# A router with experts and a Mamba scan on one core: softplus in two functions, the first low rows sent sooner, and a tile of one B product made by GpSimd

## The reference

```python
# layer 0: a router picks 2 of 4 experts for each pixel
logits = tokens @ router_w.T + router_b;  gates = softmax of the two largest
out = sum(gates[e] * (gelu(tokens @ fc1_w[e].T + fc1_b[e]) @ fc2_w[e].T + fc2_b[e]));  x = x + scale * out
# layer 1: LayerNorm over channels, then the same Mamba block on the 4096 pixels forwards and backwards
xr, z = split(x_norm @ W_in);  xr = silu(causal_conv4(xr) + conv_b)       # 192 channels
dbl = xr @ W_xproj;  dt = softplus(dbl[:6] @ W_dt + b_dt);  B, C = dbl[6:22], dbl[22:38]
h = exp(dt * A) * h + (dt * xr) * B;  y = sum_n(h * C)                    # 192 x 16 states, step by step
y = (y + xr * D) * silu(z);  out = (y_fwd + y_rev) @ W_out * 0.5 + x
```

## Time and profile before

| | before |
|---|---|
| median of 3 runs | 5707.55 us |
| profiled execution | 5689.39 us, of which the span on the core is 5687.6 us |
| granted TensorE clock, mean | 0.821 |
| VectorE, GpSimd, TensorE, ScalarE busy | 92%, 90%, 79%, 78% of the span |
| scans | 3072, the first at 218.1 us |
| a pair of bodies in the middle images | forward 84.8 us, reverse 86.2 us |

### The profile page before, as it was taken

How to read it: one execution, slowest core, us unless ns; L and a number is a source line. 1 busy time by engine, 2 the same in 40 slices (tenths; PEclk the granted TensorE clock), 3 DMA queues, 4 the chain that set the end, 5 groups by cost and what they waited for, 6 DMA issues and landing times.

```text
span 5687.6 us, 47285 instructions
## 1 busy us (share of the span) xinstructions
PE 4485.6 (79%) x12946; PEld 1323.8 (23%) x12946; DVE 5245.5 (92%) x4449; ACT 4435.3 (78%) x6737; POOL 5145.4 (90%) x2121
## 2 busy tenths in 40 slices
PE   8777887778877888778887788777887788876676
PEld 3222222222222222222222222222222222221121
DVE  2699999999999999999999999999999999999998
ACT  3578888888888878878888888888888888887675
POOL 0499999999999999999999999999999999999998
PEclk8887887788887888888887788887888788887777
DMA  4476777677776777776777777676777777776776
GB/s 112 112 176 166 174 178 168 164 175 174 170 178 162 170 176 174 167 176 165 173 175 166 170 177 172 167 178 162 173 179 166 171 173 170 173 173 160 173 174 153
DMA packets 417569, 954.68 MB, mean 168 GB/s; under 512 B 56624, under 2 KB 56873, under 8 KB 382744
## 3 DMA queue, kind: packets, MB, share of 16 engines
q1 hardware_dynamic: 417304, 951.65, 70.4%
HBM read 770.08 MB, written 181.36 MB: 167 GB/s over the span
## 4 chain that ended last, share of the span: by engine, by line
POOL 27%; DVE 18%; PE 17%; ACT 14%; DMA 12%; issue 9%; SPq 2%; POOLq 0%; DVEq 0%; ACTq 0%
POOL X L1467 17%; DVE X L1361 13%; POOL X L1458 8%; PE ps L747 4%; DVE X L1345 4%; PE ps L726 4%; ACT ps L1079 4%; DMA bc_d<-bc 3%; PE ps L781 3%; DMA lo_d<-bc 2%; DMA lo<-lo_d 2%; DMA out<-xf 2%; DMA hi_d<-S 2%; DMA xf<-x_d 1%; DVE hid L1325 1%
## 5 line engine op out<-in xcount | busy, mean ns | idle before, releaser
L1467 POOL TENSOR_TENSOR X<-X,cR 128x2048 f32<-128x2048 f32 x768 | 3477.8, 4528 | 61.8
L1361 DVE TENSOR_TENSOR_SCAN X<-ps,carry,X 128x512 f32<-128x512 f32 x2688 | 3262.6, 1263 | 137.4 <-ACT ps L1079 136.3
L1079 ACT ACTIVATE ps<-hi,amat 128x512 f32<-128x512 f32 x2048 | 1377.3, 682 | 672.9 <-DVE X L1361 668.8
L781 PE MATMUL ps<-X,red 128*32 128x512 f32 x6144 | 911.1, 671 | 486.8 <-POOL X L1467 486.2
L1458 POOL TENSOR_TENSOR X<-lo,bR 128x2048 f32<-128x2048 f32 x258 | 1167.8, 4527 | 68.9 <-DMA lo<-lo_d 68.2
L1345 DVE TENSOR_TENSOR X<-hi,ps 128x2048 f32<-128x2048 f32 x512 | 1159.8, 2265 | 49.1 <-PE ps L781 49.0
L747 PE MATMUL ps<-win,w_u 97*128 97x512 f32 (+1 forms) x2080 | 1159.3, 710 | 2.9 <-ACT xr L1034 0.9
L1079 ACT ACTIVATE ps<-lo,amat 128x512 f32<-128x512 f32 x1026 | 687.3, 677 | 121.5 <-DVE X L1361 104.3
L762 PE MATMUL ps<-xr,wd 128*96 128x512 f32 (+1 forms) x520 | 432.1, 928 | 276.0 <-ACT xr L1034 218.9
L747 PEld LDWEIGHTS ps<-win,w_u 97*128 97x128 f32 (+1 forms) x2080 | 390.0, 198 | 693.5 <-issue 690.5
L1361 DVE TENSOR_TENSOR_SCAN X<-ps,X 128x512 f32<-128x512 f32 x384 | 445.5, 1205 | 47.0 <-ACT ps L1079 36.5
(11 more groups left out here) (125 smaller groups left out, 3969.2 us busy)
## 6 DMA issues: line engine op xcount, KB each, us to landing
hi<-hi_d SPq DMA_DIRECT2D x516, 512.0 KB, 8.2
bR<-bc_d SPq DMA_DIRECT2D x516, 256.0 KB, 4.6
cR<-bc_d SPq DMA_DIRECT2D x516, 256.0 KB, 7.3
lo<-lo_d SPq DMA_DIRECT2D x516, 256.0 KB, 4.6
hi_d<-S SPq DMA_DIRECT2D x258, 256.0 KB, 8.3
y_d<-yf SPq DMA_DIRECT2D x128, 256.0 KB, 10.4
yb<-y_d SPq DMA_DIRECT2D x112, 256.0 KB, 9.9
win<-xn_d SPq DMA_DIRECT2D x130, 195.1 KB
```

The source lines that it names most:

```text
L781: last = mm(p_y[GRP * j:GRP * j + GRP, :], red[:, :], X[:, slot(par, s), j, :], start=False, stop=(s in (LOW - 1, NB - 1)), skip_group_che ...
L1079: A_(p_a[i % RING][:, :], dt, ACT.Exp, scale=amat[:, column(i):column(i) + 1]).then_inc(s_exp, 1)
L1361: V.tensor_tensor_scan(h, a, h, 0.0 if head else carry[:, i:i + 1], ALU.mult, ALU.add).then_inc(s_scan, 1)
L1467: G.tensor_tensor(batch(par, s), batch(par, s), quads(cR, par, s), ALU.mult).then_inc(s_hc, 1)
```

## The change

1. **Softplus in two functions.** ScalarE makes Exp(x) from PSUM and then Ln(1 + e). Abs is gone. `make_dt` takes max(x, min(Ln, 17.5)). ScalarE does Exp and Ln of the low rows at tile 0, the copy of B and C and Exp of the high rows at tile 1, Ln of the high rows at tile 2. VectorE does `make_dt` at tiles 3 and 5.
2. **Prologue.** SyncE sends B and C rows, B loads, low store and low loads ahead of the piece's store and the C loads. VectorE does the two `make_dt` between `gate_hidden` tiles. GpSimd does the two low products of body 0 ahead of `normalise`.
3. **A shared batch.** In even bodies and in reverse bodies the third high product (batch 4) is VectorE's for three tiles, and GpSimd makes the fourth, between `normalise` and `times_c` 3. The scan of tile 19 waits for it.

```diff
+        SHARED = LOW + 2
+        def shared(odd, rev):
+            return rev == 1 or not odd
...
             for j in range(LAST):
-                store_x2(0, j, j, PROLOGUE.by[f"p{j}"])
                 if j == AT_D0:
                     store_bc(0, 0)
                     load_b(0, 0)
-                    load_c(0)
                     store_low(0, 0)
                     load_low(0, 0)
+                store_x2(0, j, j, PROLOGUE.by[f"p{j}"])
+                if j == AT_D0:
+                    load_c(0)
                     store_high(0, 0)
                     load_high(0, 0)
...
-                A_(LOG[k], begin(u, f"D{k}")[0:ROWS_OF[k], :], ACT.Abs).then_inc(s_sp[k], 1)
-                act.wait_ge(s_sp[k], b * 3 + 1)
-                A_(LOG[k], LOG[k], ACT.Exp, scale=-1.0).then_inc(s_sp[k], 1)
+                A_(LOG[k], begin(u, f"D{k}")[0:ROWS_OF[k], :], ACT.Exp).then_inc(s_sp[k], 1)
...
+                    if i == 0:
+                        softplus_log(1, n + 1)
                     if i == 1:
                         copy_bc(u, n + 1)
-                        softplus_log(1, n + 1)
-                    if i == 2:
                         softplus_start(0, u, n + 1)
-                    if i == 3:
+                    if i == 2:
                         softplus_log(0, n + 1)
...
+                tiles = BATCH - (s == SHARED and shared(par, rev))
-                V.tensor_tensor(X[:, slot(par, s), :, :], hi[:, par, HIGH:2 * HIGH, :],
-                                p_b[:, :].unsqueeze(1).to_broadcast([P, BATCH, CH]), ALU.mult).then_inc(s_bh, 1)
+                V.tensor_tensor(X[:, slot(par, s), 0:tiles, :], hi[:, par, HIGH:HIGH + tiles, :],
+                                p_b[:, :].unsqueeze(1).to_broadcast([P, tiles, CH]), ALU.mult).then_inc(s_bh, 1)
...
+                if s == SHARED and j == BATCH - 1 and shared(par, rev):
+                    dve.wait_ge(s_bq, quarters(n))
...
-                    if i == 4:
+                    if i == 3:
                         make_dt(1, u, n + 1)
+                    if i == 5:
+                        make_dt(0, u, n + 1)
                     if i == 6:
-                        make_dt(0, u, n + 1)
...
+            def times_b_shared(n, par):
+                pool.wait_ge(s_hi, n * 64 + 64)
+                same, b = summed_before(par, SHARED)
+                pool.wait_ge(s_sum, n * NB + (NB * same + b + 1))
+                G.tensor_tensor(X[:, slot(par, SHARED), BATCH - 1, :], hi[:, par, 2 * HIGH - 1, :],
+                                bR[:, par, SHARED - LOW, :], ALU.mult).then_inc(s_bq, 1)
...
                 if second:
                     normalise(pc - 1)
+                if shared(odd, rev):
+                    times_b_shared(n, par)
                 times_c(n, 3, par, rev)
```

More of the change, by code:

```diff
@@ L21 @@
 LN_EPS = 1e-5
+SURE = 17.5
 BATCH = 4
@@ L369, in moe_mamba @@
         s_bh = sem("dBx_high_ready")
+        s_bq = sem("dBx_quarter_ready")
         s_scan = sem("h_ready")
@@ L393, in moe_mamba, with quarters @@
         block = ctx.enter_context(nc.Block())
+        SHARED = LOW + 2
+        def shared(odd, rev):
+            return rev == 1 or not odd
+        def quarters(n):
+            return sum(shared(b % 2, b % BODIES // NCH) for b in range(n + 1))
         def body_number(img, q, rev, odd):
@@ L1048, in softplus_start @@
                 act.wait_ge((s_shi, s_slo)[k], b * 32 + 32)
-                A_(LOG[k], begin(u, f"D{k}")[0:ROWS_OF[k], :], ACT.Abs).then_inc(s_sp[k], 1)
-                act.wait_ge(s_sp[k], b * 3 + 1)
-                A_(LOG[k], LOG[k], ACT.Exp, scale=-1.0).then_inc(s_sp[k], 1)
+                A_(LOG[k], begin(u, f"D{k}")[0:ROWS_OF[k], :], ACT.Exp).then_inc(s_sp[k], 1)
             def softplus_log(k, b):
-                act.wait_ge(s_sp[k], b * 3 + 2)
+                act.wait_ge(s_sp[k], b * 2 + 1)
                 A_(LOG[k], LOG[k], ACT.Ln, bias=1.0).then_inc(s_sp[k], 1)
@@ L1150, in body @@
                         softplus_start(1, u, n + 1)
+                    if i == 0:
+                        softplus_log(1, n + 1)
                     if i == 1:
                         copy_bc(u, n + 1)
-                        softplus_log(1, n + 1)
+                        softplus_start(0, u, n + 1)
                     if i == 2:
-                        softplus_start(0, u, n + 1)
-                    if i == 3:
                         softplus_log(0, n + 1)
@@ L1330, in make_dt, with times_b @@
             def make_dt(k, u, b):
[L1332 to L1337, removed]
+                dve.wait_ge(s_sp[k], b * 2 + 2)
+                free(u, f"D{k}", V.scalar_tensor_tensor(LOG[k], LOG[k], SURE, p_w[u.at[f"D{k}"][0]][0:ROWS_OF[k], :],
+                                                        op0=ALU.min, op1=ALU.max))
+            def times_b(n, h, par, rev):
                 s = LOW + h
+                tiles = BATCH - (s == SHARED and shared(par, rev))
                 if h == 0:
@@ L1380, in _ @@
                 for m in range(HT):
+                    if j == AT_D0 and m in (1, 3):
+                        make_dt(int(m == 1), by["d0"], 0)
                     gate_hidden(m, u)
@@ L1390, in _ @@
                 if j == AT_D0:
-                    for k in (1, 0):
-                        make_dt(k, by["d0"], 0)
                     gates(2, 1, IMGS)
@@ L1412, in body @@
                     if i in (7, 11, 15, 19):
-                        times_b(n, i // 4 - 1, par)
+                        times_b(n, i // 4 - 1, par, rev)
                     scan(n, i, rev, par, before != rev)
@@ L1473, in _ @@
                         times_x(k, PROLOGUE.by["d0"], 0)
-                normalise(j)
                 if j == AT_D0:
@@ L1477, in _ @@
                         times_b(0, s, 0)
+                normalise(j)
             def body(img, q, rev, odd, last, before, pc, u, even, ahead):
```

## The result

The changed kernel is slower: 5734.96 us in the median of 9 runs (5719.49 to 5748.91) against 5702.18 us for the kernel before (9 runs, 5698.69 to 5715.38). The ratio is 1.0057, 95% interval 1.0045 to 1.0069, or +32.5 us. The forecast was +41 us, ratio 1.0072. The profiled execution of after took 5731.37 us, 42 us more than that of before.

The account below looks back on a forecast made before the run. VectorE and GpSimd, both full, were taken to hand the path to and fro. Forward pairs +29, reverse pairs +21 and prologue -8.5 gave +41.5 us on a 5707.55 us median: 5748.5 us, forecast 5719 to 5790, full range 5672 to 5792.

Parts of the forecast that it names:

- The reverse pair: Two reverse bodies: two GpSimd tiles add 2.44 us, waits and slack take part; +0.65 us remains, +21 us over 32 pairs.
- the wait for rows: GpSimd's low product waiting for its rows: 0.75 us used up per reverse pair, unchanged in forward pairs.
- The slack of the even reverse bodies: Spare time ahead of the gate multiply in even reverse bodies: about 0.7 us, all used up by the tile.
- The forward pair: Even and odd forward body: tile +1.22 us, less 0.3 from softplus, so +0.9 us; +29 us over 32 pairs.
- A sign that I had named for the loop: Odd forward bodies: VectorE's idle time ahead of the fourth high product would rise by 0.5 us or more.
- the loop: Forward pair paced through GpSimd's list, TensorE's projection and VectorE's tiles back to the third C product; takes the tile's 1.22 us.
- The other sign: Odd forward bodies: the loop would be wrong if TensorE idled less than before ahead of its second sum.
- The 0.3 us back from the softplus: Even forward bodies, tiles 0 to 6: softplus no longer holds up tile 5's scan, saving 0 to 0.57 us, taken as 0.3.
- The prologue: Start of the kernel: low rows sent earlier, first scan at 209.5 us, saving 8.5 us (bounds 4 to 10).
- VectorE's own piece is 1.3 us late: Prologue: two `make_dt` within the earlier piece push VectorE's last gate product, ending at 207.8 us, back by about 1.3 us.
- Rival D: All bodies: two-function softplus shortens each by ScalarE's 1.26 us, 161 us in all; chance 0.03, inside the faster side.
- Rival A: VectorE is the bound, GpSimd's waits take the tile; 64 reverse bodies save 0.57 us each, giving 5663 us; chance 0.2.

Follow-up runs that it names:

- spare_rev: Changed kernel with GpSimd's tile in reverse bodies alone, written to a buffer nobody reads, VectorE making all four tiles: 1.0038 of before.
- share_fwd: Changed kernel with GpSimd's tile in even forward bodies alone, at its place behind the normalise: 1.0024 of before.
- soft_only: Kernel before with only the softplus in two functions and its new places: 0.9991 of before.
- pro_only: Kernel before with only the prologue's new order: 0.9988 of before.
- the early place: Changed kernel with GpSimd's tile moved ahead of the third C product, where GpSimd waits for the scan of tile 11: 0.9970 of before.
- gates_spread: Changed kernel without the shared tile, VectorE's eight gate instructions done between the fifth piece's `gate_hidden` tiles: 0.9980 of before.
- no_share: Changed kernel with VectorE making all four tiles in every body, so softplus and prologue only: 0.9977 of before.
- no_share_2: The same kernel as `no_share`, measured again on another chip: 0.9993 of before.

## Why the prediction was right, step by step

- **Direction and size** were right: +41 us forecast, +32.5 measured, on a chance of 0.62 for slower. That the sum came so near is in part luck: the forward term was too large by 7 to 12 us, the reverse term too small by 8 to 18 us, and the two errors cancel.
- **The prices** held. 1274 ns for GpSimd's tile (1271 forecast), 0.53 us saved for 0.57. GpSimd's busy time rose by 116 us (117 forecast), VectorE's fell by 42 (51 to 55 forecast: 8 us went to the two long instructions of the prologue), ScalarE's by 144 (160 forecast).
- **The reverse pair** was +0.65 us forecast, and is 0.9 by the traces and 1.2 by the times. The mechanism was right: the gate multiply is tight nearly everywhere in after, and no worth of VectorE's relief is seen in `spare_rev`. The term that was mis-sized is the wait for rows. I took 0.75 us of it as used up in a reverse pair, from a mean over all bodies; from before to after it fell by 0.37 us there, and by 1.0 us in a forward pair, where I had left it untouched. The slack of the even reverse bodies (0.7 us) was used up as forecast: from the third C product of an odd body to the next one the mean grew by only 0.3 us (42.6 to 42.9). From that of an even body to that of the odd one it grew by 1.1 us (43.7 to 44.8), nearly the whole tile. The half of the odd bodies that were tight doesn't explain this. With each body's own slack, up to the delay, the mean comes to 0.27 us of the 0.35 us that I used. In five traces with the new softplus and no reverse tile, that stretch is already 44.0 to 44.3 us, so 0.3 to 0.6 us of the 1.1 isn't the tile's, whether it is the softplus's or scatter.
- **The forward pair** was +0.9 us forecast and is 0.5 by the traces and 0.6 to 0.7 by `share_fwd`. A sign that I had named for the loop failed: VectorE's idle time ahead of the fourth high product of odd bodies was to rise by 0.5 us or more. Its mean is 1.24 us in before, 0.9 to 1.3 us in the ten other kernels without the late forward tile, and 0.81, 0.85 and 1.10 us in the three with it. The other sign held: TensorE's idle time ahead of its second sum in odd bodies did not fall (0.53 us in before, 0.76 in after). So the loop isn't shown to take the tile. What is shown in its place is the longer way from tile 6 to tile 12 of the odd body, behind ScalarE's copy of y, and a wait for rows that gave way by 1.0 us a pair. The 0.3 us back from the softplus came and went: from the first scan of an even forward body to that of tile 6 the mean fell from 8.74 to 8.39 us in `soft_only`, but from there to tile 12 it rose from 12.02 to 12.58 us. ScalarE reaches its copy of y in these bodies earlier and waits 1.5 us instead of 0.3 for the last sum of the body before, which comes no sooner.
- **The prologue** was -8.5 us forecast and is -3.0 by the first scan, -7 us (-1 to -13) by the time of `pro_only`, whose own first scan comes 1.3 us sooner. The step that failed is "VectorE's own piece is 1.3 us late". It was 7.3 us late (its last gate product ends at 215.1 for 207.8 us): 4.2 us by the end of the fifth piece, most of it at the lower clock, and 3 us because two instructions stood still for 8.4 us beside GpSimd, part of which VectorE would have waited for TensorE anyway. I had named no cost for running GpSimd's two products there. In the two traces without the clash and at the full clock the stretch from the fifth piece to the first scan is 10.5 us shorter than in before: there the forecast's mechanism holds.
- **Softplus**: no effect in the bodies forecast but 0.3 us in forward pairs; `soft_only` is 0.9991 with an interval that holds no change. Rival D is out.
- **Rival A** (GpSimd's waits take the tile, VectorE is the bound) fails at the place where the change put the tile, and its first half is right at another: at the early place 136 us of GpSimd's waiting for scans went, and the kernel is faster than before. Its second half, 0.57 us saved in each reverse body, is not shown at either place. The prediction named 272 us of waits as room for 117 us of work, and didn't ask what each of these waits was behind. It was not the sum of GpSimd's waits that decided, but on which side of them the new work stood.

## What to carry to other kernels

When work goes from one full engine to another, its price is set by the place in the other's list: ahead of a wait it fills the wait, behind it it delays all that the next engines need, and no total of busy or idle time shows the difference. Before giving an instruction to an engine, find its longest wait and see whether the operands are ready ahead of it. Where a price rests on a wait or a slack, read it in the part of the program where the work is added: the mean over all bodies put 0.75 us on a pair that gave 0.37, and nothing on one that gave 1.0. And look at the terms one by one when a sum comes out right, since two of them were wrong here in opposite directions.

## What the runs showed of the hardware

GpSimd's products over SBUF operands hold up VectorE's instructions of certain forms, and whole ones. The CAST of 128x896 took 0.63 us alone and 4.83 us beside a low product; the product of two SBUF operands 1.09 and 5.28 us, and GpSimd's pair of low products 10.08 us for 8.98. With the gates ahead of the low products these kept the short times; an earlier one with two SBUF operands, beside GpSimd's dt times x in `gates_spread`, took 1.78 us for 1.09. The two traces of one kernel, `no_share` and `no_share_2`, show the same without any change of the program: in the first the CAST ends before the low products begin (185.78 us), in the second it lies beside them (from 203.94 us on).

```profile
183.52 0.63 DVE L1323 CAST g<-sz 128x896 bf16<-128x896 f32 x1
```

```profile
204.84 4.82 DVE L1323 CAST g<-sz 128x896 bf16<-128x896 f32 x1
```

The high products, scans and gate products of the bodies take one operand from PSUM and run beside GpSimd at their 2.26, 1.26 and 0.67 us. The Trainium skill has it so (SBUF — State Buffer, "Who interferes with whom"): a VectorE copy or cast in a two-port mode contends with GpSimd for a shared port pair, which the first to issue holds for its whole instruction; one with two SBUF inputs contends with a GpSimd instruction that reads SBUF; one with at most one SBUF input outside these modes doesn't contend. The trace agrees, in the order too: in after the two-input product at 199.43 us, begun 0.23 us ahead of GpSimd's, kept its 1.09 us, and GpSimd's product beside it took 5.24 us for some 4.5.

The start varies between executions too: two traces of the same kernel, `no_share` and `no_share_2`, have the first scan at 194.6 and 219.3 us. The table by stage of each (stretch and its us; busy us and count of PE, PEld, DVE, ACT, POOL; granted clock, DMA share, GB/s), `no_share` first:

```profile
80.00:130.00 50.00, 47.52 (x206) 19.44 (x206) 7.63 (x18) 21.82 (x34) 1.26 (x1) 0.97 0.31 80
```

```profile
80.00:130.00 50.00, 48.89 (x137) 16.70 (x136) 7.61 (x15) 15.64 (x24) 1.26 (x1) 0.72 0.32 81
```

TensorE was busy nearly all of both stretches, but was granted 0.97 of its full clock in one and 0.72 in the other, and the recorded matmuls are 206 against 137. The start is TensorE's there. The fifth piece begins at 169.3 and at 187.5 us, 18 of the 25 us between the two first scans; its lower clock and the long instructions of the prologue make the other 7. One first scan therefore says little of a prologue's change, and the 3 us between before and after no more.
